# A new order for the middle stage, rotary halves read 64 partitions on, and sign products from two float32r parts

## The reference

```
xn = layernorm(x)
x  = x + state_space(xn) + clip((xn @ sign(W).T) * scale + bias, -100, 100)
xn = layernorm(x)
x  = x + attention_a(xn) + block_b(xn)      # attention_a: 16 heads of 16, ALiBi, causal
# block_b: h = rmsnorm(xn)*ln1; q, k, v = h @ wqkv.T (16 query heads, 4 key heads)
#          q, k = rope(q), rope(k); causal attention; x = x + attn @ wo.T;
#          h = rmsnorm(x)*ln2; the two best of 8 experts; x + their weighted sum
# rope(t) = t*cos + concat(-t2, t1)*sin, where t1, t2 are the halves of a head's 16 features
```

## Time and profile before

| what | us |
|---|---|
| median of the runs | 2414.33 (2411.44 to 2416.97, 3 runs) |
| the profiled execution | 2416.83 |
| its span | 2415.0 |
| TensorE busy | 2228.2 (92%) |
| VectorE busy | 2024.4 (84%) |
| ScalarE busy | 1534.4 (64%) |
| GpSimd busy | 673.3 (28%) |

### The profile page before, as it was taken

One profiled execution on the slowest core, in us unless ns is written; L12 is line 12 of the kernel. 1 busy time (PEld: TensorE's weight loads), 2 busy tenths in 40 slices (PEclk: granted clock), 3 DMA queues, 4 the chain that ended last, 5 costly groups with the idle time before them and its releaser, 6 DMA issues. The chain is left out here.

```text
span 2415.0 us, 47953 instructions
## 1 busy us (share of the span) xinstructions
PE 2228.2 (92%) x15890; PEld 1283.8 (53%) x15891; DVE 2024.4 (84%) x5163; ACT 1534.4 (64%) x2973; POOL 673.3 (28%) x993
## 2 busy tenths in 40 slices
PE   4599997999999999999999999999998884999997
PEld 2355544444544444444444544444543662888886
DVE  7777655899999999999999999999992564777775
ACT  3133321568888888888888888888888452444443
POOL 5422100223223223223223223222211264233333
PEclk8799996899999999999999999999999996999999
DMA  4167864747535545424334423423131895344443
GB/s 165 64 184 199 229 192 84 118 73 142 104 88 104 110 89 100 103 68 93 73 75 92 74 72 87 83 68 83 59 96 49 286 311 209 74 81 83 79 81 72
DMA packets 175822, 271.55 MB, mean 112 GB/s; under 512 B 53657, under 2 KB 126505, under 8 KB 169781
## 3 DMA queue, kind: packets, MB, share of 16 engines
q0 software_dynamic: 45984, 137.68, 28.2%
q1 hardware_dynamic: 124596, 121.03, 17.1%
q10 hardware_dynamic: 5044, 10.32, 1.5%
HBM read 128.77 MB, written 139.14 MB: 111 GB/s over the span
## 5 line engine op out<-in xcount | busy, mean ns | idle before, releaser
L1474 ACT ACTIVATE a_p<-banks 128x512 f32<-128x512 f32 x2176 | 1131.3, 608 | 257.6 <-PE banks L1367 206.5
L1527 DVE TENSOR_REDUCE a_mx<-banks 128x1 f32<-128x512 f32 x1536 | 944.2, 682 | 22.0 <-PE banks L1356 21.5
L1435 PE MATMUL banks<-a_p,a_v 128*32 128x512 f32 (+3 forms) x5120 | 588.9, 544 | 1.6 <-ACT a_o L1492 1.1
L1356 PE MATMUL banks<-a_k,a_q 52*128 52x512 f32 (+5 forms) x1600 | 446.7, 413 | 1.9 <-DVE a_rowtop L1524 0.3
L1367 PE MATMUL banks<-a_q,a_k 50*128 50x512 f32 (+7 forms) x1600 | 415.9, 396 | 1.1
L1524 DVE CUSTOM_DVE_ANT_0 a_masked<-banks,a_later 128x512 bf16<-128x512 f32 (+3 forms) x768 | 330.8, 485 | 18.4 <-PE banks L1356 16.7
L1367 PEld LDWEIGHTS banks<-a_q,a_k 54*128 54x128 f32 (+1 forms) x1600 | 227.0, 185 | 199.2 <-DVE a_mx L1527 95.4
L1356 PEld LDWEIGHTS banks<-a_k,a_q 52*128 52x128 f32 (+1 forms) x1600 | 224.2, 185 | 117.4 <-DVE a_mx L1527 55.5
L1356 PE MATMUL banks<-a_k,q 48*128 48x512 f32 (+6 forms) x896 | 257.9, 422 | 5.2 <-DMA a_k<-aug_rows 3.7
L1367 PE MATMUL banks<-q,a_k 50*128 50x512 f32 (+7 forms) x896 | 231.5, 402 | 1.1 <-DVE a_orow L1547 0.3
L1435 PEld LDWEIGHTS banks<-a_p,a_v 128*32 128x32 f32 x5120 | 109.3, 108 | 174.9 <-issue 125.9
(11 more groups left out here) (276 smaller groups left out, 3028.8 us busy)
## 6 DMA issues: line engine op xcount, KB each, us to landing
expert_rows<-a_zeros POOLq DMA_DIRECT2D x132, 258.0 KB, 5.3
a_k<-ka_parts POOLq DMA_DIRECT2D x42, 256.0 KB, 6.3
e_x<-expert_rows SPq DMA_DIRECT2D x72, 129.0 KB, 2.2
expert_rows<-e_y SPq DMA_DIRECT2D x72, 128.0 KB
qa_parts<-m_part SPq DMA_DIRECT2D x16, 512.0 KB, 4.3
ka_parts<-m_part SPq DMA_DIRECT2D x16, 512.0 KB, 5.1
va_tiles<-m_va SPq DMA_DIRECT2D x8, 1024.0 KB, 4.5
qb_parts<-m_part SPq DMA_DIRECT2D x16, 512.0 KB, 3.8
```

What stands on the lines that cost most here:

```text
L1356: ins = pe.matmul(ps[bank][:, col:col + w], q_op[r % 3][part, p, qt * P:(qt + 1) * P], keys_of(r, k0)[part, kp, k0:k0 + w], start=True, st ...
L1435: ins = pe.matmul(ps_o[VW * h:VW * h + VW, c0:c0 + w], v_op[o][:, kt, hk * VW:hk * VW + VW], prob[:, (at + slot) % NPB, col:col + w], star ...
L1474: nc.scalar.activation(prob[:, (t * NSC + n) % NPB, :], ps[bank][:, :], ACT.Exp, scale=SCALE).then_inc(s_ex, 1)
L1527: ins = v.tensor_reduce(top, ps[bank][:, :], AX.X, ALU.max)
```

## The change

- The weights of the swapped features are no longer multiplied. GpSimd puts the features of q and k for block b in another order once (feature index first, head last; the 4 key heads doubled to 8), so that one group of 128 holds the first half of each head in partitions 0 to 63 and the second in 64 to 127. `rope` multiplies the group by cos as before, and reads its halves 64 partitions on for the sine product, in two instructions of 64 partitions. Three groups per block are left of six (`NPR` is 10 instead of 13), and the key group has 128 rows.
- The sign products take float32r operands: GpSimd's `sign_parts` makes a rounded part and a remainder of the tokens, and `signs` multiplies both, eight products in place of four.
- `form_h` moves from VectorE to ScalarE, `squares` writes into `h`.
- The order changes on every engine: `signs` is a step of its own at the end of `both`, u for block `blk + 2` is formed at the end of VectorE's `both(blk)`, `turn_xn` is split and moved forward, `low` steps move.
- The stored layout of q and k of block b and the tables of cos and sin change with it; the attention's loads read the same rows in another order.

```diff
+            def sign_parts(blk, before):
+                high, low = signed
+                whole = xnT[:, blk // NBB, :, blk % NBB * BT:(blk % NBB + 1) * BT]
+                pool.wait_ge(s_f, blk * KD)
+                nc.gpsimd.tensor_copy(high[:, :, :], whole).then_inc(s_zero, 1)
+                pool.wait_ge(s_zero, before + 1)
+                nc.gpsimd.tensor_tensor(low[:, :, :], whole, high[:, :, :].bitcast(F32), ALU.subtract).then_inc(s_zero, 1)
+
             x_rows(0)
             x_rows(1)
             carry(1)
+            sign_parts(1, 0)
+            pool.wait_ge(s_w, NW * 16)
+            for k in range(KD):
+                ins = nc.gpsimd.tensor_copy(
+                    wb[:, k, D:2 * D].rearrange("p (m d h) -> p m d h", m=KD, d=HD),
+                    wb[:, k, 0:D].rearrange("p (m h d) -> p m d h", m=KD, d=HD))
...
             for blk in range(2, NBLK):
                 x_rows(blk)
                 if blk + 1 < NBLK:
                     carry(blk + 1)
+                sign_parts(blk, blk * 2 + 2)
...
+            def signs(blk):
+                pe.wait_ge(s_hT, blk * KD)
+                pe.wait_ge(s_zero, 2 if blk == 1 else blk * 2 + 4)
+                for k in range(KD):
+                    for c in range(KD):
+                        for i, part in enumerate(signed):
+                            ins = pe.matmul(ps[2 + k][:, :], w_raw[:, c, k * P:(k + 1) * P], part[:, c, :],
+                                            start=(c + i == 0), stop=(c + i == KD))
+                    ins.then_inc(s_f, 1)
...
 # TensorE, both(blk)
-                pe.wait_ge(s_pd, blk * NDVE + 1)
-                for n in range(2):
-                    features(n, wa, n * P, P, xT)
+                pe.wait_ge(s_pd, max(blk * NDVE, 1))
+                features(0, wa, 0, xT)
+                pe.wait_ge(s_pd, blk * NDVE + 1)
+                features(1, wa, P, xT)
                 if more:
                     turn_u(blk + 1)
...
+                if more:
+                    turn_xn(blk + 1, 0)
                 pe.wait_ge(s_lo, blk * NS + 3)
-                features(6, wb, 0, P, hT)
+                features(6, wb, D, hT)
+                if more:
+                    turn_xn(blk + 1, 1)
                 pe.wait_ge(s_lo, blk * NS + 4)
-                features(7, wb, D, P, hT)
-                if more:
-                    turn_xn(blk + 1)
+                features(7, wb, D + P, hT)
                 pe.wait_ge(s_pd, blk * NDVE + 2)
-                features(8, wb, P, P, hT)
-                pe.wait_ge(s_pd, blk * NDVE + 3)
-                features(9, wb, D + P, P, hT)
+                features(8, wb, 0, hT)
+                if ahead:
+                    pe.wait_ge(s_xT, blk * KD + 2 * KD)
+                    first_products(blk + 2)
                 if more:
                     turn_h(blk + 1)
-                pe.wait_ge(s_pd, blk * NDVE + 4)
-                features(10, wb, 2 * D, KV * HD, hT)
-                features(11, wb, 2 * D + KV * HD, KV * HD, hT)
...
+                pe.wait_ge(s_pd, blk * NDVE + 3)
+                values(9, wb, 2 * D + 2 * KV * HD, KV * HD, hT, range(TPB))
                 if ahead:
-                    pe.wait_ge(s_xT, blk * KD + 2 * KD)
-                    pe.wait_ge(s_hT, blk * KD + 2 * KD)
-                    first_products(blk + 2)
-                pe.wait_ge(s_pd, blk * NDVE + 5)
-                values(12, wb, 2 * D + 2 * KV * HD, KV * HD, hT, range(TPB))
+                    signs(blk + 2)
...
 # ScalarE, both(blk), after squares(blk + 1)
-                    take_xT(blk + 1)
+                    take_xT(blk + 1, 0)
+                    rms(blk + 1)
+                    take_xT(blk + 1, 1)
+                    form_h(blk + 1)
                 high(4)
-                high(5)
                 if more:
                     take_hT(blk + 1)
+                if ahead:
+                    scale_ffn(blk + 2, 0)
+                high(5)
                 high(6)
+                if ahead:
+                    scale_ffn(blk + 2, 1)
...
 # VectorE, rope(m)
-                    ch.did(v.tensor_tensor(xf[i][0:n, :], ps[BANK[a % 4]][0:n, :], cos[0:n, tok:tok + BT], ALU.mult))
-                    v.tensor_tensor(rot[0:n, :], ps[BANK[r % 4]][0:n, :], sin[0:n, tok:tok + BT],
+                    ch.did(v.tensor_tensor(xf[i][:, :], from_[:, :], cos[:, tok:tok + BT], ALU.mult))
+                    if blk or m > 4:
+                        dve.wait_ge(s_xf, blk * 3 + (m - 4))
+                    ch.did(v.tensor_tensor(rot[0:HALF, :], from_[HALF:P, :], sin[0:HALF, tok:tok + BT], ALU.mult))
+                    v.tensor_tensor(rot[HALF:P, :], from_[0:HALF, :], sin[HALF:P, tok:tok + BT],
                                     ALU.mult).then_inc(s_pd, 1)
...
 # VectorE, both(blk): low(0), add_residual, low(1), normalise, low(2), low(3), va, mean_square, then
                 rope(4)
                 if more:
-                    form_h(blk + 1)
+                    inverse_rms(blk + 1)
                 rope(5)
+                if ahead:
+                    begin_u(blk + 2, 0)
                 low(4)
-                low(5)
+                if ahead:
+                    begin_u(blk + 2, 1)
                 rope(6)
-                low(6)
...
+                low(5)
+                low(6)
+                if ahead:
+                    for k in range(KD):
+                        form_u(blk + 2, k)
```

More of the change, by code:

```diff
@@ L490, in middle @@
         xf = [sb(f"m_xf{i}", [P, BT]) for i in range(2)]
-        rots = [sb(f"m_rot{i}", [P, BT]) for i in range(2)]
-        part = [sb(f"m_part{m}", [P, 2, BT], F32R) for m in range(NS)]
+        rot = sb("m_rot", [P, BT])
+        parts = [sb(f"m_part{m}", [P, 2, BT], F32R) for m in range(NS - 1)]
+        parts.append(parts[2])
         s_w = M["s_mid_weights"]
@@ L589, in _ @@
                     sp.wait_ge(s_lo, blk * NS + (m + 1))
[L590 to L596, removed]
+                    dram = (M["qa_d"], M["qa_d"], M["ka_d"], M["ka_d"], M["qb_d"], M["qb_d"], M["kb_d"])[m]
+                    row = b * D + (m % 2) * P if m < 6 else b * P
+                    sp.dma_start(dram[:, row:row + P, tok:tok + BT].rearrange("a f t -> f a t"),
+                                 parts[m][:, :, :].bitcast(F32)).then_inc(s_pst[m], 16)
                 sp.wait_ge(s_va, blk * 2 + 2)
@@ L665, in alone @@
                 keep_going(pe, M, ps[4], 20)
-                turn_xn(0)
+                for k in range(KD):
+                    turn_xn(0, k)
                 keep_going(pe, M, ps[4], 6)
@@ L670, in alone @@
                 pe.wait_ge(s_xT, KD)
-                pe.wait_ge(s_hT, KD)
                 first_products(1)
+                signs(1)
             def both(blk, more, ahead):
@@ L684, in both @@
                 for n in range(2, 4):
-                    features(n, wa, n * P, P, xT)
+                    features(n, wa, n * P, xT)
                 pe.wait_ge(s_lo, blk * NS + 1)
@@ L843, in mean_square, with inverse_rms @@
                 v.tensor_scalar(msv[:, :], ms[:, :], 1.0 / D, LN_EPS, ALU.mult, ALU.add).then_inc(s_ms, 1)
-            def form_h(blk):
+            def inverse_rms(blk):
                 dve.wait_ge(s_rsd, blk + 1)
-                ch.did(v.reciprocal(rs[:, 1, :], sd[:, 1, :]))
-                ch.settle()
-                for j in range(TPB):
-                    ins = v.tensor_scalar(h[:, j, :], xn2[blk % 2][:, j, :], rs[:, 1, j:j + 1], None, ALU.mult)
-                ins.then_inc(s_h, 1)
-            def alone():
-                for stage in (form_u, add_residual, normalise, mean_square, form_h):
-                    stage(0)
+                v.reciprocal(rs[:, 1, :], sd[:, 1, :]).then_inc(s_ms, 1)
+            def alone():
+                for k in range(KD):
+                    begin_u(0, k)
+                    form_u(0, k)
+                add_residual(0)
+                normalise(0)
+                mean_square(0)
+                inverse_rms(0)
+                for k in range(KD):
+                    begin_u(1, k)
+                    form_u(1, k)
             def both(blk, more, ahead):
@@ L860, in low @@
                 def low(m):
-                    n = P if m < 6 else KV * HD
-                    high = part[m][0:n, 0, :].bitcast(F32)
+                    high = parts[m][:, 0, :].bitcast(F32)
                     dve.wait_ge(s_hi, blk * NS + (m + 1))
                     if m < 4:
-                        ins = v.scalar_tensor_tensor(part[m][:, 1, :], ps[BANK[m]][:, :], ba[:, m:m + 1], high,
+                        ins = v.scalar_tensor_tensor(parts[m][:, 1, :], ps[BANK[m]][:, :], ba[:, m:m + 1], high,
```

165 lines of the change are left out of this document (95 added, 70 removed).

## The result

The changed kernel took 2393.6 us (median of 4 runs, 2386.46 to 2393.89), the kernel before in the same session 2415.65 (2411.44 to 2417.28): a ratio of 0.9903, 95% interval 0.9889 to 0.9918. The profiled execution took 2393.55 us, its span 2391.3. Run again on another occasion the same kernel gave 2383.78 us (2381.08 to 2390.99, 5 runs) beside 2412.83, 0.9892 [0.9876, 0.9908]. The forecast was 2387 us, the range 2364 to 2406.

The account below looks back on a forecast made before the run. TensorE's count of products was taken to bound the middle. Gains of 15.2 us in the loop, 4.1 at the start and 7.9 at the end made 27.2: 2389.6 us profiled, 2387 against the median, range 2364 to 2406.

Parts of the forecast that it names:

- TensorE's part: TensorE's products in a middle block: 24.2 us after the change, the float32r signs about 2.2 of it.
- VectorE's part: VectorE's work in a middle block: 24.0 us from 23.1, h removed, each rotation 0.68 us longer.
- The clean loop: Dependency loop through TensorE and VectorE from u's transposes to the next u: 24.5 us a block without GpSimd's interference.
- The splitting beside VectorE: End of blocks 0 to 4: GpSimd's token splitting stalls VectorE's SBUF work by 3.0 us, bounds 0 and 3.8.
- The clock: Behind the idle gap before u's transposes TensorE's clock falls, costing 1.9 us more in each such block.
- The carries: GpSimd's carries in three more heads, blocks 1 to 3, hold up variance and normalisation: 0.8 us each.
- The loop's sum: First rotation of block 0 to that of block 6: 173.9 us instead of 189.1, gain 15.2.
- The start: Up to block 0's first rotation: u formed ahead brings it to 134.3 us, gain 4.1.
- The end: From block 6's first rotation to the middle's last store: 31.6 us instead of 39.5, gain 7.9.
- The engines don't meet: Rival, chance 0.25: no stall or slow clock in the middle, 2360 to 2369 us, with part of it up to 2378.
- Dearer: Rival, chance 0.15: shifted halves cost over 0.68 us or carry stall and slow clock add fully; about 2399 us.
- the DMA: Rival, chance 0.05: transfers take over in the middle, late stores hold buffers, intervals stay at 31.5 us, no change.

Follow-up runs that it names:

- the longer bridge: The changed kernel with 56 instead of 20 idle products between the middle and the attention: 2388.6 us, 0.9897.
- The rotary part alone: The kernel before with three feature groups instead of six and rotation by halves; order, sign products and h as before: 2423.76 us, 1.0049.
- one step of the new order of TensorE: The kernel before with the rotary change, state products before h's transposes and float32 sign products after the values: 2391.42 us, 0.9911.
- the kernel with float32 signs: The changed kernel with four float32 sign products as before and no splitting on GpSimd: 2368.32 us, 0.9821.

## Why the prediction was right

The prediction was right in the result (2393.6 us, inside 2364 to 2406 and inside the 2378 to 2396 of the forecast, 6.6 us above the 2387 named) and in the mechanism: what bounds the middle, the stall, its cause and its place. Several terms were mis-sized, and their errors largely cancel. The middle gained 31.2 us where 27.2 were forecast, and 7.5 of them were lost behind it in the profile; that the total came this near is partly luck.

- **What bounds it.** The middle was bound by TensorE's count, and the gain arises there: the last store of the middle went from 366.99 to 335.83, 31.2 us. TensorE's share of the middle didn't fall to the 80% foretold, though, but to 89% (148.3 us of the 166.1 in six intervals); the blocks were shorter than forecast, and slow products count as busy.
- **TensorE's part**, predicted 24.2 us a block with 2.2 for the signs: 2.10 us for the signs, and 24.07 us of busy time over 278 to 303 us, where the one clean interval (24.8 us) lies. Right.
- **VectorE's part**, 2.62 us for a rotation: 2.85 from its start to that of the next instruction. The second half product starts 0.73 us after the first, where the two full products of before were 0.61 apart. Neither the 64 partitions nor the shift doubles anything. The Trainium skill ("VectorE: DVE Perf Modes", section "Two Vector instructions with no wait between them") says that an instruction that starts to read or write in another quadrant (a group of 32 partitions) than the last one that read or wrote the same memory is held until all earlier ones have finished; the trace agrees (0.73 against 0.61). No run with unshifted halves was made. The sum for a block, 24.0 us, was 22.7 in the clean interval: it started from the 23.1 of a block with a carry, while blocks of before without one had 22.0.
- **The clean loop**, 24.5 us: 24.8.
- **The splitting beside VectorE**, 3.0 us: two low parts took 3.71 instead of 1.29, so 2.42. The gap was predicted at 3.3 us and is 3.35, but as 3.0 on top of 0.3, where it is 2.42 on top of 0.93: two errors that cancel. The cause is shown by three runs: with the splitting moved, the gap goes to 0.93 and the stall appears elsewhere; with its subtraction doubled, the gap is 5.50; without the splitting, it is 0.86 in one of the six blocks and not there in the others.
- **The clock**, 1.9 us in each of five blocks: right in kind, wrong in the number. It fell in three of five behind the same gap, in the second run and in the longer bridge's in all five. Without a carry, an interval with a low clock is 28.5 to 29.0 us, one without 27.2 to 27.4, so 1.2 to 1.8 us; the one of 30.1 us with the longer bridge makes it 2.9. Filling the gap keeps the clock at 1.00.
- **The carries**, 0.8 us in three heads: in two heads only (the next one, from 223.99 on, lies beside rotations that go on at 0.69 us), and there 1.4 us with the clock up and 0.3 to 0.7 beside a low one. I had added the two terms; they overlap.
- **The loop's sum**, 173.9 us for six intervals: 166.1. Clock and carries were to make 11.9 us and made 4.8 (1.9, 1.6, 1.3, 0 and 0 over 27.3); the stall 15 and made 12.5 (27.3 less the clean 24.8, five times); the loop itself was 1.7 longer. In the second run, with five low clocks, the sum was 169.2.
- **The start**, 4.1 us gained: 1.3. In proportion this term failed most. I allowed 2 us for GpSimd; in block 0 two carries and one splitting lie end to end from 118.4 to 132.3, and u's addition took 3.08, the variance 1.83 and the normalisation 5.07 us, together 7.7 over their 0.69, 0.17 and 1.38. U's transposes came at 121.1, not at 122, but the way from there to the first rotation took 16.0 us instead of 12.2. Without the splitting the first rotation comes at 132.99, before the 134.3 of the forecast.
- **The end**, 7.9 us gained: 6.8 (32.7 from the last block but one to the store, 31.6 predicted).
- **"Everything after the middle only shifted"**: not in one profile. Of 31.2 us gained 23.7 arrive at the end of the span. Most of the loss lies in the first attention step, whose load of `a_later` was issued 30.1 us earlier and whose first store 25.4 us earlier (442.36 against 467.79). That step took 96.5 us before, 101.2 in this profile and 96.3 in the second one of the same kernel, and 94.7 to 100.7 in the other nine experiments. So it varies by itself by some 5 us. Over all that follows the middle two profiles of the changed kernel differ by 14.3 us, nearly twice the 7.5 that were lost, and the forecast's sum of 27.2 us met the measured 22 and 29 with that scatter in it. What sets it stays open; the longer bridge didn't lower it.

**The rivals.** "The engines don't meet" was wrong for the kernel, but right in its price: without the splitting it takes 2368 us, inside the 2360 to 2378 that I gave it. "Dearer" and "slower" didn't occur; the clock recovers within a head. As to the DMA, stores did hold a part's buffer up (ScalarE waited 1.0, 0.8 and 2.9 us for `kb_parts`), but no wait of TensorE between two first rotations goes back to them.

What I didn't ask is what each part is worth. The sum credits the removed products as if any order could use them. The rotary part alone loses 11 us, because the products it removes were the cover of h; with one step of the new order of TensorE it gains 22, with the whole new order 44 (by the kernel with float32 signs). And the float32r signs, which look like a gain by TensorE's rows (1.3 us a block), cost 17 to 20 us of it (0.9892 and 0.9903 against 0.9821).

## What to carry to other kernels

Before removing work from the engine that bounds a stage, look for what that work covers: here three product groups less made the kernel slower, until other products were put into the wait for h. Moving work to GpSimd is not free while VectorE works in SBUF on the critical loop: price it by what VectorE would be doing at that moment, and add what the idle gap does to TensorE's clock. And weigh a part of a change alone: the version without the splitting beats the whole by 0.7 to 0.8%.

## What the runs showed of the hardware

- GpSimd holds up VectorE's arithmetic on operands in SBUF for nearly its own length (3.71 instead of 1.29 us, 5.50 instead of 1.38, 2.56 instead of 0.41); instructions that read PSUM beside GpSimd's kept their 0.69 us. Statistics from SBUF (`bn_stats`, 1.41 us at 123.20, beside the copy of the splitting) and a reciprocal (0.16 at 189.15) were not held up either; the prediction had taken every instruction with all operands in SBUF to be stopped. It goes both ways: an addition of GpSimd's that met the addition of a rotation took 1.73 us instead of 1.27 (226.14). The Trainium skill ("SBUF — State Buffer", section "SBUF: two separate sides") limits the exclusive lock, on VectorE's side, to instructions in a two-port mode or with two inputs in SBUF. The trace agrees for additions and subtractions of two tensors in SBUF, which were held up (3.71 for 1.29 us), and for `bn_stats`, which reads one tensor there and wasn't. Clip and normalisation read one tensor in SBUF too and were held up; whether they ran in a two-port mode the trace doesn't show.
- Behind the same idle gap of 3.35 us TensorE's granted clock fell in three of five blocks in one profile and in all five in two others. Where it fell, it could be a microsecond late: at 183.28 the transposes took 1.09 us at full clock, and the features behind them 5.29 instead of 3.60.
- Two VectorE products of 64 partitions that read the half opposite to the one they write take 0.69 us each, as one of 128, and start 0.73 apart.
